# The scatter phase of a mixture-of-experts layer: W2 on 32x32 tiles of the matrix engine, block transposes on the vector engine

## The chip, the cores and the metric

The kernel runs on one core of one Trainium2 chip. The metric is the device time of one execution in microseconds. The engines are PE (matrix products; PEld is its weight load), DVE (vector), ACT (scalar), POOL (GpSimd) and SP, which here only issues transfers; 16 DMA engines move data.

## The reference

Tokens are 16,384 rows of 512. The output is `x + attention(xn) + ffn(xn)`, where `xn` is the layer norm of `x`. The attention part (a chunked state-space scan with projections) isn't touched except in how its result is stored. The feed-forward part is a mixture of 128 experts (32 x 4 sets) of inner size 32, in which each group of 32 consecutive tokens is treated by itself:

```
logits = einsum('bntd,des->bntes', grouped, Wc) + bc          # and a tiny tie breaker
perm = (logits == max over t)                                 # one-hot: each expert picks one token of the group
permuted = einsum('bntd,bntes->bnesd', grouped, perm)
inner = relu(einsum('bnesd,esdf->bnesf', permuted, W1) + b1)
result_permuted = einsum('bnesf,esdf->bnesd', inner, W2) + b2
result = einsum('bnesd,bntes->bntd', result_permuted, perm)   # back to the tokens that were picked
```

There are 512 groups. Everything is in fp32.

## The kernel before

Three phases follow each other. **Attention** runs over 64 tiles of 256 tokens and stores the normalised tokens (`xn_dram`), the residual sum (`part_dram`) and the one-hot rows (`permT_dram`, bf16). **Gather** runs over blocks of `GB` = 64 groups: PE picks each expert's token (`pick`, L1462), applies W1 (`apply_w1`, L1486), DVE clamps (`clamp_acc`, L1420), POOL adds b1 (L1376), and the inner results go to `inner_dram`. **Scatter**, which the change rewrites, applies W2 and b2 and sends the results back to the tokens.

The scatter works on `SG` = 128 groups at a time and a quarter of the 512 columns (`KD` = 4), 16 steps in all, each of `NW` = 8 units; there are 128 units. A unit has 16 experts:

- `apply_w2` (L1716): for each expert, W2 [32 inner x 128 columns] is the stationary operand and the inner results [32 x 128 groups] move; four experts lie on the four row tiles of PE. The result has columns on partitions and groups along the free axis.
- `add_b2` (L1693): DVE empties PSUM, adds b2 (here a per-partition value) and sorts into `resT[.., group, expert]`, two instructions of 1024 elements. For the first units ACT takes a quarter of it (`add_b2_last`, L1668).
- `transpose_results` (L1748), one step later: for each group PE transposes [128 columns x 128 experts], four into a PSUM bank, and ACT copies the bank (L1679) to `res`.
- `gather_results` (L1761): for each group `res` [128 experts x 128 columns] moves and the one-hot matrix `perm` [128 experts x 32 tokens] is stationary, on one of four column tiles.
- `write_out` (L1725): DVE adds the residual and SP stores (L1615).

SP issues the loads of W2 (L1576, one piece of 256 KB per unit), inner results (L1585), residual (L1612) and one-hot rows (L1589), which POOL unfolds from bf16 to fp32 (L1657). PE's order is written out by hand: the transposes of 16 groups, W2 of the unit `LAG` = 9 ahead, the 16 gathers:

```
for u in range(LAG, UNITS + LAG):
    first = UT * (u - LAG)
    for n in range(first, first + UT):
        transpose_results(n)
    if u < UNITS:
        apply_w2(pe, u)
    for n in range(first, first + UT):
        gather_results(n)
```

In the profile an fp32 product is two matmul instructions, one of type fp32r or a transpose is one. Tiles of the scatter have names that begin with `s_`, those of the gather with `g_`.

Of the kernel before, what the change touches and what calls it, by code (L numbers as in the profile page):

```python
# [55 lines left out]
SG = 128  # L56
NSET = TOK // (SG * GRP)
STL = SG * GRP // P
NW = 8
QW = NQ // NW  # L60

# [30 lines left out]
def attention_phase(nc, io, keep, sems):  # L92
# [250 lines left out]
    def sync_program(sync, gather):  # L343
# [877 lines left out]
def gather_phase(nc, io, keep, sems, att):  # L1221
# [25 lines left out]
    inner = [sb(f"inner{i}", [P, NQ, GB], at=AT_INNER + 8192 * i) for i in range(2)]  # L1247
# [78 lines left out]
    def store_inner(eng, b, piece):  # L1326

        quads = slice(PQ * piece, PQ * piece + PQ)
        eng.wait_ge(biased, 2 * b + 1 + 2 * piece // PIECES)
        eng.dma_start(inner_dram[b][:, quads, :], inner[b % 2][:, quads, :]).then_inc(inner_out[b % 2], 16)  # L1330

    def sync_program(sync, scatter):
# [10 lines left out]
        for e in range(4 * LAST):  # L1343
# [11 lines left out]
            if b == NGB - 1 and w % 4 == 3:  # L1355
                scatter["load_first"](sync, w // 4)
        for piece in range(PIECES // 2):
            store_inner(sync, NGB - 1, piece)
        for w in range(2):
            scatter["load_w2_next"](sync, w)  # L1360
        for piece in range(PIECES // 2, PIECES):
            store_inner(sync, NGB - 1, piece)
        for w in range(2, 4):
            scatter["load_w2_next"](sync, w)
# [5 lines left out]
    def gpsimd_program(pool):  # L1370
        for b in range(NGB):
            for i in range(2):
                pool.wait_ge(acc_cp, 2 * b + i + 1)
                quads = slice(2 * QW * i, 2 * QW * (i + 1))
                half = inner[b % 2][:, quads, :]
                nc.gpsimd.tensor_tensor(half, half, b1[:, quads].unsqueeze(2).to_broadcast([P, 2 * QW, GB]),  # L1376
                                        ALU.add).then_inc(biased, 1)
# [17 lines left out]
    def scalar_program(act, scatter):  # L1395
        for n in range(LAST):
            b, k = divmod(n, KD)
            for tq in range(2 if n == 0 else 0, 4):
# [10 lines left out]
                if b > 0 and 0 <= w - 5 < PIECES:  # L1409
                    store_inner(act, b - 1, w - 5)  # L1410
        for u in range(4):
            scatter["add_b2_last"](act, u)

    def vector_program(dve, scatter):
        def clamp_acc(b, i):
            dve.wait_ge(acc_ps, 4 * b + 2 * i + 2)
            if i == 0:
                wait(dve, inner_out[b % 2], 16 * PIECES * (b // 2))
            lower = b1neg[:, 2 * QW * i:2 * QW * (i + 1)].rearrange("p (j q) -> p j q", j=2)
            nc.vector.tensor_tensor(inner_view(b, i), acc_bank[:, halves(i), :, :],  # L1420
                                    lower.unsqueeze(3).to_broadcast([P, 2, QW, GB]), ALU.max).then_inc(acc_cp, 1)
# [96 lines left out]
def scatter_phase(nc, io, keep, sems, att, gat):  # L1518
# [11 lines left out]
    STEPS = NSET * KD  # L1530
    UT = STL // NW
    UNITS = STEPS * NW
    LAG = NW + 1
    EW = 4 * QW
    NC = 4
    CT = SG * GRP // NC
    NPART, NOUT = 2, 3

    w2 = sb("w2", [P, NW, QW, P], at=AT_XNT)
    b2 = sb("b2", [P, KD, EX], at=AT_PERM0)  # L1540
    ident = sb("ident", [P, P], at=AT_PERM0 + 2048)
    inner = sb("inner", [P, NQ, SG], at=AT_ONEHOT)
    permT = [sb(f"permT{i}", [P, CT], BF16, at=AT_PERM1 + 2048 * i) for i in range(2)]
    perm = sb("perm", [P, SG * GRP], at=AT_XN3)
# [340 lines left out]
```

## Time and profile before

| | |
|---|---|
| runs | 3000.07 us median of 3 (2998.5 to 3001.02) |
| profiled execution | 3002.6 us from the first to the last instruction |
| scatter, from the first transpose to the last gather product | 2488.7 to 2998.8 us |
| busy in the stretch 2485 to 3003 us (518 us) | PE 511, PEld 442, DVE 363, ACT 268, POOL 29 us; DMA 72% |
| busy in the gather phase, 2070 to 2480 us (410 us) | PE 319, PEld 274, DVE 181, ACT 148, POOL 29 us; DMA 46% |

The profile is one execution; its span is 2.5 us above the median of the runs. A line number (L1748) is a line of the kernel before. "Issue" as a releaser is time in which the engine waited for nothing that the profile shows. Busy time is the union of the instructions' durations; the mean of one is longer than the step between two where instructions overlap.

### The profile page before, as it was taken

What the parts mean: (1) busy time and instruction counts of PE and PEld (TensorE: products, weight loads), DVE (VectorE), ACT (ScalarE), POOL (GpSimd) and SP (SyncE); (2) the same over time, 40 slices, a digit from 0 to 9 for tenths busy, and PEclk for the clock granted to TensorE, in tenths of its full rate; (3) what the DMA queues carried; (4) which work ended last, traced back from release to release, by engine and by line L of the source; (5) the groups of instructions that cost most, each with busy time, mean ns of one, the idle gap of its engine ahead of it and who ended that gap; (6) DMA issues with size and microseconds to landing.
All of it is one profiled execution on the core that took longest, in us unless ns stands there. A gap on an engine that the chain in (4) does not pass through costs nothing.

```text
span 3002.6 us, 134681 instructions
## 1 busy us (share of the span) xinstructions
PE 2871.7 (96%) x59324; PEld 2453.1 (82%) x59324; DVE 2053.3 (68%) x2982; ACT 1713.5 (57%) x3751; POOL 1430.4 (48%) x2287
## 2 busy tenths in 40 slices
PE   8999999999999999999999999996787879999999
PEld 6888888888888888888888888885666668888887
DVE  5777777777777777777777777775444447777775
ACT  5665666666656666666566666663333335555555
POOL 4666676766666767667667666672010101101010
PEclk9999999999999999999999999998999999999999
DMA  4222222222222222222222222216444437877765
GB/s 150 77 74 71 77 78 75 76 74 77 74 71 79 76 76 76 70 80 74 72 79 74 80 71 71 81 46 214 131 134 119 115 110 217 235 218 223 225 206 156
DMA packets 372550, 328.99 MB, mean 110 GB/s; under 512 B 62960, under 2 KB 284656, under 8 KB 371328
## 3 DMA queue, kind: packets, MB, share of 16 engines
q1 hardware_dynamic: 362016, 310.21, 35.6%
q8 instruction: 469, 7.68, 1.1%
q10 hardware_dynamic: 9952, 10.17, 1.1%
q14 instruction: 113, 0.93, 0.1%
HBM read 206.96 MB, written 113.31 MB: 107 GB/s over the span
## 4 chain that ended last, share of the span: by engine, by line
PE 90%; DVE 4%; issue 3%; DMA 1%; SPq 1%; POOL 1%; ACT 0%; ACTq 0%; DVEq 0%; POOLq 0%
PE a_proj L992 40%; PE a_mix L992 11%; PE s_rt L1748 8%; PE g_pick_ps L1462 5%; PE a_scan L1106 5%; PE s_w_ps L1716 5%; PE s_rt L1761 4%; DVE g_picked L1393 3%; PE a_scan L1083 3%; PE a_scan L1070 2%; PE g_acc_ps L1486 2%; PE a_mix L1058 2%; PE a_misc L1050 1%; PE a_misc L1124 1%; DMA part_dram<-res 1%
## 5 line engine op out<-in xcount | busy, mean ns | idle before, releaser
L992 PE MATMUL a_proj<-wdh,xTh 128*128 128x512 f32 x1024 | 420.9, 411 | 5.0 <-issue 3.1
L1679 ACT COPY s_res<-s_rt 128x512 f32<-128x512 f32 x512 | 262.9, 601 | 245.8 <-PE s_rt L1748 245.8
L992 PE MATMUL a_proj<-wdh,xTl 128*128 128x512 f32 x1024 | 402.0, 393 | 0.0
L992 PE MATMUL a_proj<-wdl,xTh 128*128 128x512 f32 x1024 | 400.0, 391 | 1.5 <-issue 1.5
L824 DVE COPY_PREDICATED scan_in<-mask,a_scan 64x512 f32<-64x512 uint32 x512 | 382.3, 747 | 16.0
L1693 DVE TENSOR_TENSOR s_resT<-s_w_ps,s_b 128x1024 f32<-128x1024 f32 (+1 forms) x252 | 293.1, 1205 | 136.4 <-PE s_w_ps L1716 136.4
L465 POOL TENSOR_TENSOR dx<-xs,d_row 64x512 f32<-64x512 f32 x256 | 330.3, 1290 | 15.1
L640 ACT ACTIVATE scan_in<-CT,hsel 64x128 f32<-64x128 f32 x1024 | 326.0, 388 | 4.9
L473 POOL TENSOR_TENSOR yv<-yt,dx 128x512 f32<-128x512 f32 x128 | 188.6, 1473 | 292.8 <-DVE yt L864 292.8
L604 ACT ACTIVATE raw<-a_proj,rs 128x272 f32<-128x272 f32 x128 | 62.5, 488 | 427.6 <-PE a_proj L992 427.6
L1393 DVE COPY g_picked<-g_pick_ps 128x1024 f32<-128x1024 f32 x128 | 156.7, 1224 | 216.3 <-PE g_pick_ps L1462 216.3
L884 DVE SCALAR_TENSOR_TENSOR res<-a_mix,rms,x 128x512 f32<-128x512 f32 x127 | 95.4, 751 | 270.9 <-PE a_mix L992 258.6
L456 POOL TENSOR_TENSOR scan_in<-CT,hsel 64x512 f32<-64x512 f32 x256 | 269.0, 1051 | 10.0
L1389 ACT COPY g_picked<-g_pick_ps 128x1024 f32<-128x1024 f32 x128 | 129.6, 1012 | 248.4 <-PE g_pick_ps L1462 247.8
L1748 PE MATMUL s_rt<-s_ident,s_resT 128*128 128x128 f32 x2048 | 254.7, 278 | 0.9 <-DVE s_resT L1693 0.5
L616 ACT ACTIVATE xs<-a_proj,rs 64x512 f32<-64x512 f32 x256 | 174.8, 683 | 125.0 <-PE a_proj L992 123.4
L1748 PEld LDWEIGHTS s_rt<-s_ident,s_resT 128*128 128x128 f32 x2048 | 219.0, 140 | 31.6 <-issue 25.1
L992 PEld LDWEIGHTS a_proj<-wdh,xTh 128*128 128x128 f32 x1024 | 192.2, 188 | 47.5 <-issue 10.8
L992 PEld LDWEIGHTS a_proj<-wdh,xTl 128*128 128x128 f32 x1024 | 192.3, 188 | 45.4 <-issue 1.9
L992 PE MATMUL a_proj<-xTh,wth 128*128 128x256 f32 x768 | 222.1, 289 | 0.0
L992 PEld LDWEIGHTS a_proj<-wdl,xTh 128*128 128x128 f32 x1024 | 193.0, 188 | 35.2 <-issue 2.9
L992 PE MATMUL a_proj<-xTh,wtl 128*128 128x256 f32 x768 | 216.3, 282 | 0.0
(153 smaller groups left out, 7104.4 us busy)
## 6 DMA issues: line engine op xcount, KB each, us to landing
x<-in_x_dram SPq DMA_DIRECT2D x128, 256.0 KB, 2.7
xn_dram<-xn SPq DMA_DIRECT2D x128, 256.0 KB, 2.4
part_dram<-res SPq DMA_DIRECT2D x128, 256.0 KB, 2.5
g_xn<-xn_dram SPq DMA_DIRECT2D x512, 64.0 KB, 2.3
s_w<-in_w_dram SPq DMA_DIRECT2D x128, 256.0 KB, 4.1
s_part<-part_dram SPq DMA_DIRECT2D x128, 256.0 KB, 3.9
out_dram<-s_out SPq DMA_DIRECT2D x128, 256.0 KB, 3.0
xr<-in_xT_dram SPq DMA_DIRECT2D x126, 256.0 KB, 2.8
```

The source lines that it names most:

```text
L456: nc.gpsimd.tensor_tensor(c_places(1, w), src, sel, ALU.mult).then_inc(cs_cp[1], 1)
L465: nc.gpsimd.tensor_tensor(dx[rows_, :], xs[c][n % 4][rows_, :, :].rearrange("t h d -> t (h d)"), d_row[rows_, :], ALU.mult).then_inc(dx_cp, 1)
L473: nc.gpsimd.tensor_tensor(yv[:], yt[:], dx[:], ALU.add).then_inc(yv_cp, 1)
L616: last = nc.scalar.activation(xs[c][n % 4][rows_, :, :], proj[0][rows_, :].rearrange("p (h d) -> p h d", h=H), ACT.Copy, scale=inv(n, rows_))
L640: last = nc.scalar.activation(dst[:, :, j, :], CT[own, n % 4, :, 0:CH], ACT.Copy, scale=hsel4[own, j:j + 1])
L824: nc.vector.copy_predicated(dst, mask[rows_, :].unsqueeze(1).unsqueeze(1).to_broadcast([CH, 4, 2, CH]), src).then_inc(mt_cp, 1)
L992: last = nc.tensor.matmul(out, lhs[a], rhs[c], start=(k == 0 and n == 0), stop=(k == nk - 1 and n == 2))
L1106: last = nc.tensor.matmul(out, scan_in[c][:, h, i:i + 32], xs[c][n % 4][:, h, :], start=True, stop=True)
L1393: nc.vector.tensor_copy(picked_view(n, tq, 1), pick_view(1)).then_inc(pick_cp[1], 1)
L1679: nc.scalar.copy(res[:, n % 4, :, :], rt_bank[:, n % 3, :, :]).then_inc(res_cp, 1)
L1693: last = nc.vector.tensor_tensor(resT[m % 2][j][:, :, sets].rearrange("p n (q r) -> p n q r", r=4)[:, :, :, 0:r], w2_place(u)[:, 0:r, :, j ...
L1748: last = nc.tensor.transpose(rt_bank[:, n % 3, g, :], resT[m % 2][j][:, place, :], ident[:])
```

## The change

The scatter takes `SG` = 32 groups at a time and half of the columns (`NH` = 2, `DH` = 256): 32 steps of four units, 128 units as before. A unit has 32 experts.

- `apply_w2`: the inner results [32 inner x 32 groups] are the stationary operand and W2 [32 x 256 columns] moves. Row tile r holds expert r of a quad and column tile c another quad, so that the 16 tiles of 32 x 32 hold 16 experts. The result has groups on partitions (one column tile's experts in each 32) and columns along the free axis.
- `evict`: ACT copies it to `stage` in two instructions of 1024 elements, without b2.
- Once a step DVE turns `stage` into `turned` with four block transposes of 2048 elements per partition (`nc.vector.transpose` turns every 32 x 32 block of partitions and the innermost axis; both innermost axes step by 256 elements, 1 KB), after which experts are on partitions.
- `gather_results`: b2, split into two fp32r parts [128 experts x 256 columns], moves over the one-hot matrix of 128 tokens (four one-pass products a unit), and onto this sum the eight groups' gather products of 256 columns are added.
- ACT copies the sum out (`copy_out`), POOL adds the residual, SP stores.

W2's half (4 MB) stays in SBUF for 16 steps and is loaded twice in all. PSUM is used as three pairs of banks for W2 results and two banks for the output. In the gather phase the inner results are laid out in sets of 32 groups, so that the clamp and the addition of b1 are two instructions each in place of one. The residual is stored in halves of 256 columns. The core of the diff:

```diff
-SG = 128
+SG = 32
 NSET = TOK // (SG * GRP)
-STL = SG * GRP // P
-NW = 8
-QW = NQ // NW
+NH = 2
+DH = D // NH
...
+    inner = [sb(f"inner{i}", [P, GB // SG, NQ, SG], at=AT_INNER + 8192 * i) for i in range(2)]
...
+                for h in range(GB // SG):
+                    half = inner[b % 2][:, h, quads, :]
+                    last = nc.gpsimd.tensor_tensor(half, half, b1[:, quads].unsqueeze(2).to_broadcast([P, 2 * QW, SG]), ALU.add)
+                last.then_inc(biased, 1)
...
+            lower = b1neg[:, 2 * QW * i:2 * QW * (i + 1)].unsqueeze(2).unsqueeze(3)
+            for h in range(GB // SG):
+                last = nc.vector.tensor_tensor(inner_view(b, i, h), acc_view(i, h),
+                                               lower.to_broadcast([P, 2 * QW, GPT, SG // GPT]), ALU.max)
+            last.then_inc(acc_cp, 1)
...
-        w2_bank = ctx.enter_context(nc.psum_tensor("s_w2_ps", [P, 4, QW, SG], F32))
-        rt_bank = ctx.enter_context(nc.psum_tensor("s_rt", [P, 4, QW, SG], F32))
-    out_bank = rt_bank[:, 3, :, :].rearrange("p q n -> p (q n)")
+        bank = ctx.enter_context(nc.psum_tensor("s_ps", [P, 8, 2, DH], F32))
...
+    QB = 4
+    UNITS = NH * NSET * QB
+    STEPS = NH * NSET
+    LAG = 2 * QB
+    CT = SG * GRP
+    DT = DH // 4
+    NPART, NOUT, NINNER = 3, 3, 3
...
+    def pair(u, h):
+
+        first = h if u < 4 else (2 * u + h) % 3
+        return slice(2 * first, 2 * first + 2)
...
+        for u in range(UNITS + LAG + 1):
+            m, i = divmod(u, QB)
+            if u < UNITS and (m == NSET - 1 or i == QB - 1):
+                sync.wait_ge(w2_ps, u + 1)
+            if m == NSET - 1:
+                load_w2(sync, 1, i)
+            if i == QB - 1 and m + NINNER < STEPS:
+                load_inner(sync, m + NINNER)
+            v = u - LAG - 1
+            if v >= 0:
+                store(v)
+                if v + NPART < UNITS:
+                    load_part(v + NPART)
+                m, x = divmod(v, QB)
+                if x == 1 and m + 3 < STEPS:
+                    sync.wait_ge(perm_ready, m + 2)
+                    load_perm(sync, m + 3)
+            elif u == LAG - 1:
+                sync.wait_ge(perm_ready, 1)
+                load_perm(sync, 2)
...
+        def spread_perm(m):
+            pool.wait_ge(perm_in[m % 2], 16 * (m // 2 + 1))
+            wait(pool, out_ps, QB * (m - 1))
+            nc.gpsimd.tensor_tensor(perm[m % 2][:], permT[m % 2][:], ones[:].to_broadcast([P, CT]), ALU.mult).then_inc(perm_ready, 1)
...
+        for v in range(UNITS):
+            m, x = divmod(v, QB)
+            pool.wait_ge(out_cp, v + 1)
+            pool.wait_ge(part_in[v % NPART], 16 * (v // NPART + 1))
+            nc.gpsimd.tensor_tensor(out[v % NOUT][:], out[v % NOUT][:], part[v % NPART][:], ALU.add).then_inc(out_add, 1)
+            if x == 0 and m + 1 < STEPS:
+                spread_perm(m + 1)
...
+    def evict(act, u):
+
+        m, i = divmod(u, QB)
         act.wait_ge(w2_ps, u + 1)
-        for q in range(QW):
-            e = EW * w + 4 * q + 3
-            for j in range(2):
-                last = nc.scalar.activation(resT[m % 2][j][:, :, e], w2_place(u)[:, 3, q, j * GB:(j + 1) * GB],
-                                            ACT.Identity, bias=b2[:, m % KD, e:e + 1])
-        last.then_inc(res_last, 1)
+        wait(act, turn_cp, 4 * (m - 1))
+        places = stage[m % 2][:, 8 * i:8 * i + 8, :].rearrange("p (j r) d -> p r j d", r=4)
+        for h in range(2):
+            nc.scalar.copy(places[:, 2 * h:2 * h + 2, :, :], bank[:, pair(u, h), :, :]).then_inc(w2_cp, 1)
...
+        def copy_out(v):
+            act.wait_ge(out_ps, v + 1)
+            wait(act, out_done[v % NOUT], 16 * (v // NOUT))
+            nc.scalar.copy(out[v % NOUT][:], bank[:, 6 + v % 2, :, :]).then_inc(out_cp, 1)
...
+    def vector_program(dve):
+        for m in range(STEPS):
+            dve.wait_ge(w2_cp, 2 * QB * (m + 1))
+            wait(dve, out_ps, QB * (m - 1))
+            for y in range(4):
+                cols = slice(DT * y, DT * y + DT)
+                nc.vector.transpose(turned[m % 2][:, :, cols].rearrange("p n d -> p d n"),
+                                    stage[m % 2][:, :, cols].rearrange("p e d -> p d e")).then_inc(turn_cp, 1)
...
+    def apply_w2(pe, u):
+
+        m, i = divmod(u, QB)
+        k, s = divmod(m, NSET)
+        if s == 0:
+            pe.wait_ge(w2_in[i], 16 * (k + 1))
+        if i == 0:
+            pe.wait_ge(inner_in[m % NINNER], 16 * (m // NINNER + 1))
+        if u == 4:
+            pe.wait_ge(gat["acc_cp"], 2 * NGB)
+        wait(pe, w2_cp, 2 * u if u < 4 else 2 * u - 1)
+        for j in range(2):
+            for c in range(4):
+                for r in range(4):
+                    rows_ = slice(ES * r, ES * r + ES)
+                    dst = bank[32 * c:32 * c + 32, pair(u, r // 2), :, :][:, r % 2, j, :]
+                    last = nc.tensor.matmul(dst, inner[m % NINNER][rows_, 8 * c + 2 * i + j, :], w2[rows_, i, 2 * c + j, :],
+                                            start=True, stop=True)
+        last.then_inc(w2_ps, 1)
...
+        def gather_results(v):
+            m, x = divmod(v, QB)
+            cols = slice(m // NSET * DH, (m // NSET + 1) * DH)
+            if x == 0:
+                pe.wait_ge(perm_ready, m + 1)
+                pe.wait_ge(turn_cp, 4 * (m + 1))
+            wait(pe, out_cp, v - 1)
+            dst = bank[:, 6 + v % 2, :, :]
+            for t in range(2):
+                tile = slice((2 * x + t) * P, (2 * x + t + 1) * P)
+                for n in range(2):
+                    nc.tensor.matmul(dst[:, t, :], perm[m % 2][:, tile], b2[n][:, cols], start=(t == 0 and n == 0), stop=False,
+                                     skip_group_check=True)
+            for t in range(2):
+                for g in range(GPT):
+                    tok = (2 * x + t) * P + GRP * g
+                    last = nc.tensor.matmul(dst[GRP * g:GRP * g + GRP, t, :], perm[m % 2][:, tok:tok + GRP].bitcast(F32),
+                                            turned[m % 2][:, g * (SG // GPT) + 2 * x + t, :], start=False, stop=True,
+                                            skip_group_check=True)
...
+            for t in range(2):
+                for g in range(GPT):
+                    tok = (2 * x + t) * P + GRP * g
+                    last = nc.tensor.matmul(dst[GRP * g:GRP * g + GRP, t, :], perm[m % 2][:, tok:tok + GRP].bitcast(F32),
+                                            turned[m % 2][:, g * (SG // GPT) + 2 * x + t, :], start=False, stop=True,
+                                            skip_group_check=True)
             last.then_inc(out_ps, 1)
 
-        pe.wait_ge(small_in, 32)
-        for u in range(4, LAG):
-            apply_w2(pe, u)
-        for u in range(LAG, UNITS + LAG):
-            first = UT * (u - LAG)
-            for n in range(first, first + UT):
-                transpose_results(n)
+        pe.wait_ge(b2_lo, 1)
+        for u in range(4, UNITS + LAG):
             if u < UNITS:
                 apply_w2(pe, u)
-            for n in range(first, first + UT):
-                gather_results(n)
+            if u >= LAG:
+                gather_results(u - LAG)
...
-        w2=L0_ffn_W2.reshape(NW, QW, 4, KD, P, ES).transpose(3, 0, 2, 5, 1, 4).reshape(KD, NW, P, QW, P),
-        b2=L0_ffn_b2.reshape(EX, KD, P).transpose(2, 1, 0),
+        w2=L0_ffn_W2.reshape(4, 4, 2, 4, NH, DH, ES).transpose(4, 1, 3, 6, 0, 2, 5).reshape(NH, 4, P, 8, DH),
+        b2=L0_ffn_b2.reshape(EX, D),
```

## Rows read from the trace of the kernel before

**Rows 1.** The page: span, busy time by engine, granted clock in 40 slices, the chain.

```profile
span 3002.6 us, 134681 instructions
...
PE 2871.7 (96%) x59324; PEld 2453.1 (82%) x59324; DVE 2053.3 (68%) x2982; ACT 1713.5 (57%) x3751; POOL 1430.4 (48%) x2287
...
PEclk9999999999999999999999999998999999999999
...
PE 90%; DVE 4%; issue 3%; DMA 1%; SPq 1%; POOL 1%; ACT 0%; ACTq 0%; DVEq 0%; POOLq 0%
```

**Rows 2.** One tile, s_rt: count, ns min/median/max, first and last start.

```profile
L1761 PE MATMUL s_rt<-s_res,s_perm x4096: 269/273/298, 2492.3 to 2998.8; 128*32 128x128 f32 x196
...
L1748 PE MATMUL s_rt<-s_ident,s_resT x2048: 272/273/332, 2488.7 to 2997.5; 128*128 128x128 f32 x187
```

**Rows 3.** Windows of the gather and the scatter: busy time (matmuls), clock, DMA share, GB/s.

```profile
2070.00:2480.00 410.00, 319.32 (x12467) 274.21 (x12465) 180.89 (x152) 148.13 (x172) 28.53 (x15) 0.98 0.46 127
...
2485.00:3003.00 518.00, 510.98 (x10016) 441.56 (x10016) 362.93 (x373) 267.80 (x537) 28.67 (x16) 1.00 0.72 212
```

**Rows 4.** Timeline of the scatter, 2700 us: start, duration, engine, line, count.

```profile
2700.25 1.99 PE L1748 MATMUL s_rt<-s_ident,s_resT 128*128 128x128 f32 x16
2700.94 2.05 ACT L1679 COPY s_res<-s_rt 128x512 f32<-128x512 f32 x4 [1.98 <-PE s_rt L1748]
...
2702.17 1.17 PE L1716 MATMUL s_w_ps<-s_inner,s_w 32*128 32x128 f32 x32
...
2703.27 1.08 PE L1761 MATMUL s_rt<-s_res,s_perm 128*32 128x128 f32 x32
...
2704.28 1.99 PE L1748 MATMUL s_rt<-s_ident,s_resT 128*128 128x128 f32 x16
```

**Rows 5.** Timeline of PE in the attention phase, 1012 us.

```profile
1011.94 0.69 PE L1083 MATMUL a_scan<-cexp,BT 32*64 32x128 f32 x32
...
1013.29 0.28 PE L992 MATMUL a_proj<-xTh,wtl 128*128 128x256 f32 x1
1013.41 0.27 PE L992 MATMUL a_proj<-xTh,wth 128*128 128x256 f32 x1
```

**Rows 6.** What PE waited for in the gather phase: us in total, times, longest.

```profile
PE g_pick_ps L1462 <- DVE g_picked L1393: 36.9, 72, 9.1
PE g_acc_ps L1486 <- issue: 36.4, 41, 2.3
PE g_pick_ps L1462 <- issue: 10.2, 16, 1.6
```

**Rows 7.** Timeline of ACT in the gather phase.

```profile
2334.55 1.01 ACT L1389 COPY g_picked<-g_pick_ps 128x1024 f32<-128x1024 f32 x1
2335.45 1.02 ACT L1385 CAST g_perm<-g_acc_ps 128x1024 f32<-128x1024 bf16 x1
```

**Rows 8.** Groups by line and shape of DVE: busy us, mean ns of one.

```profile
L794 DVE STREAM_TRANSPOSE rsT<-rs 128x32 f32<-128x32 f32 x64 | 12.7, 199 | 0.0
...
L920 DVE TENSOR_TENSOR wtl<-a_misc,wth 128x64 fp32r<-128x64 f32 x1 | 0.2, 217 | 0.0
```

**Rows 9.** Groups by line and shape, gather and scatter, DVE and POOL.

```profile
L1693 DVE TENSOR_TENSOR s_resT<-s_w_ps,s_b 128x1024 f32<-128x1024 f32 x238 | 280.4, 1219 | 130.9 <-PE s_w_ps L1716 130.9
...
L1725 DVE TENSOR_TENSOR s_out<-s_rt,s_part 128x512 f32<-128x512 f32 x128 | 87.1, 681 | 21.0 <-PE s_rt L1761 21.0
...
L1376 POOL TENSOR_TENSOR g_inner<-g_inner,g_b 128x1024 f32<-128x1024 f32 x16 | 30.4, 1902 | 389.4 <-DVE g_inner L1420 389.4
L1657 POOL TENSOR_TENSOR s_perm<-s_permT,s_ones 128x1024 f32<-128x1024 bf16 x16 | 30.3, 1894 | 366.6 <-PE s_rt L1761 352.7 <-DMA s_permT<-permT_dram 13.8
...
L473 POOL TENSOR_TENSOR yv<-yt,dx 128x512 f32<-128x512 f32 x2 | 2.9, 1454 | 7.2 <-DVE yt L864 7.2
```

**Rows 10.** Transfers of the scatter: count, KB each, median us to landing.

```profile
s_part<-part_dram SPq DMA_DIRECT2D x128, 256.0 KB, 3.9
out_dram<-s_out SPq DMA_DIRECT2D x128, 256.0 KB, 3.0
```

**Rows 11.** Timeline, the last clamp of the gather phase.

```profile
2480.10 1.22 DVE L1420 TENSOR_TENSOR g_inner<-g_acc_ps,g_b1neg 128x1024 f32<-128x1024 f32 x1
```

More of the change, by code:

```diff
@@ L1354, in sync_program @@
                     load_xn(sync, e // 4 + 4, e % 4, i)
-            if b == NGB - 1 and w % 4 == 3:
-                scatter["load_first"](sync, w // 4)
-        for piece in range(PIECES // 2):
+            if b == NGB - 1:
+                scatter["load_first"](sync, w)
+        for piece in range(PIECES):
             store_inner(sync, NGB - 1, piece)
[L1359 to L1364, printed above, removed]
     def negate_b1(pool):
@@ L1537, in scatter_phase @@
[L1537 to L1544, printed above, removed]
-    resT = [[sb(f"resT{i}_{j}", [P, GB, EX], at=a + 32768 * i) for j, a in enumerate((AT_W1, AT_PICKED))] for i in range(2)]
-    res = sb("res", [P, 4, GPT, P])
@@ L1547, in scatter_phase @@
[L1547 to L1553 removed]
+    QB = 4
[5 more added lines that the diff above has]
+    NPART, NOUT, NINNER = 3, 3, 3
+    w2 = sb("w2", [P, QB, 8, DH], at=AT_W1)
@@ new lines, in scatter_phase @@
+    stage = [sb(f"stage{i}", [P, EX // 4, DH], at=a) for i, a in enumerate((AT_XNT, AT_W1 + 32768))]
+    turned = [sb(f"turned{i}", [P, SG, DH], at=AT_PICKED + 32768 * i) for i in range(2)]
+    inner = [sb(f"inner{i}", [P, NQ, SG], at=a) for i, a in enumerate((AT_PERM1, AT_PERM0, AT_XN3 + 12288))]
+    perm = [sb(f"perm{i}", [P, CT], F32R, at=AT_XN3 + 4096 * i) for i in range(2)]
+    permT = [sb(f"permT{i}", [P, CT], BF16, at=AT_XN3 + 8192 + 2048 * i) for i in range(2)]
+    b2 = [sb(f"b2{n}", [EX, D], F32R, at=AT_TOP + 2048 * i) for i, n in enumerate("hl")]
@@ L1554, in scatter_phase @@
+    b2_raw = sb("b2_raw", [EX, D], at=AT_TOP + 4096)
+    ones = sb("ones", [P, 1], at=AT_TOP + 6144)
+    part = [sb(f"part{i}", [P, 2, DH]) for i in range(NPART)]
+    out = [sb(f"out{i}", [P, 2, DH]) for i in range(NOUT)]
+    b2_in = sem("b2_in")
+    w2_in = [sem(f"w2_in{i}") for i in range(QB)]
+    inner_in = [sem(f"inner_in{i}") for i in range(NINNER)]
     perm_in = [sem(f"perm_in{i}") for i in range(2)]
@@ L1610, in sync_program, with load_first @@
+    def load_first(sync, w):
+        if w == 3:
+            sync.wait_ge(gat["perm_ps"], NGB)
+            sync.dma_start(b2_raw[:], io["b2"]).then_inc(b2_in, 16)
+            for m in range(2):
+                load_inner(sync, m)
+        if w in (8, 12):
+            for i in range(2):
+                load_w2(sync, 0, w // 2 - 4 + i)
+        if w == 15:
+            for m in range(2):
+                load_perm(sync, m)
+            load_inner(sync, 2)
     def sync_program(sync):
@@ new lines, in gpsimd_program, with round_b2 @@
+        for v in range(UNITS):
[5 more added lines that the diff above has]
+                spread_perm(m + 1)
+    def round_b2(act):
+        for i in range(2):
+            act.wait_ge(att["res_out"][i], 16 * NST)
+        act.wait_ge(b2_in, 16)
+        nc.scalar.copy(b2[0][:], b2_raw[:]).then_inc(b2_hi, 1)
@@ L1699, in apply_w2 @@
-    def apply_w2(pe, u):
-        m, w = divmod(u, NW)
-        pe.wait_ge(w2_in[w], 16 * (m + 1))
-        if m % KD == 0:
-            pe.wait_ge(inner_in[w], 16 * (SG // GB) * (m // KD + 1))
-        if u == 5:
-            pe.wait_ge(gat["acc_cp"], 2 * NGB)
-        elif 5 < u < LAG:
-            pe.wait_ge(res_ready, u - 1)
-            pe.wait_ge(res_last, u - 1)
-        else:
-            wait(pe, res_ready, u)
-            wait(pe, res_last, min(u, LAG))
-        for j in range(QW):
-            for r in range(4):
-                rows_ = slice(ES * r, ES * r + ES)
-                last = nc.tensor.matmul(w2_place(u)[:, r, j, :], w2[rows_, w, j, :], inner[rows_, QW * w + j, :],
-                                        start=True, stop=True)
-        last.then_inc(w2_ps, 1)
@@ L1720, in vector_program @@
[L1720 to L1726 removed]
         for u in range(4, UNITS + LAG):
             if u < UNITS:
[L1730 removed]
+                evict(act, u)
```

194 lines of the change are left out of this document (39 added, 155 removed).

## The prediction

> **What bounds the kernel now.** I read the page first [rows 1]: 3002.6 us of span, PE busy for 96% of it at full granted clock, and the chain that ended last is 90% PE. That share is an average over three phases, so the groups by line and the windows by stage came next. The change rewrites the last phase, the scatter, which by the last two of its PE lines runs from 2488.7 us to the end [rows 2], 510 us of PE work from the first transpose to the last gather product (2998.8). In this phase PE is busy for 511 of 518 us, DVE for 363, ACT for 268 and the DMA engines for 72% [rows 3]; everyone waits for PE, and PE for nobody. A timeline shows what a unit is made of [rows 4]: 16 transposes (L1748), then 16 W2 products (L1716, two instructions each), then 16 gather products (L1761, two each). They start at 2700.25, 2702.17, 2703.27, and the next unit at 2704.28: a unit takes 4.03 us, 1.92 of them for transposes, 1.10 for W2, 1.01 for gathering. There are 128 of them, 3.985 us each on average.
>
> **How PE's time scales.** Four numbers come from [rows 4, 5]. Transposes: 15 gaps in 1.99 - 0.27 = 1.72 us, 0.115 each, one at a time. Products on four tiles (L1761): 32 starts in 1.08 - 0.27 = 0.81 us; in bursts of four that is 7 gaps of 0.116, so 128 fp32 columns occupy the four tiles for about 0.11 us and the four run together. Products on eight tiles (32 rows by 64 columns, L1083): 32 starts in 0.69 - 0.27 = 0.42 us, 3 to 4 gaps of 0.11: eight run together. A change from one tile shape to another: L1761's last start is 0.81 us after its first and the next transpose starts at 1.01, so 0.20 from last start to next start, of which 0.11 is streaming and 0.09 the change; a first burst costs up to 0.1 more (L1716 needs 0.90 us for the same 7 gaps).
>
> **The change, part by part.** *PE.* The 2048 transposes go: 1.92 us a unit. W2 now has 32 products (64 instructions) of 256 columns on sixteen tiles of 32 by 32. If sixteen run together as eight do in [rows 5], a burst of 16 lasts twice 0.109, 0.218 us, and a unit has four: the last start comes 3 x 0.218 + 0.2 (slower first burst, spread of the starts) = 0.85 us in, the next stage 0.218 + 0.09 later: 1.16 us. The bias has four one-pass products of 256 columns on the whole array; the same size starts every 0.117 us in the attention phase (1013.29, 1013.41) [rows 5]: 3 x 0.117 + 0.05 + 0.117 + 0.09 = 0.61 us. Eight gather products of 256 columns are four bursts: 3 x 0.218 + 0.05 + 0.31 = 1.01 us. A unit: 1.16 + 0.61 + 1.01 = 2.78 us in place of 3.985.
>
> The Trainium skill has a measurement for sixteen tiles (TensorE: Matmul & The Clock Gate, Part 3: Packing small matmuls, Measured speedup vs the span model): 4x4 packing gains 10.6 times, not 16. By that, a W2 burst would be an estimated 0.33 us instead of 0.218, the unit 3.2 us and the kernel some 50 us above my sum, at the upper edge of the forecast. No row of before has sixteen tiles.
>
> *Issue waits.* PE stands still for no reason that the profile shows ("issue") 57 times for 46.6 us in the gather phase [rows 6] with its 12,467 matmuls in 410 us [rows 3], 3.7 ns a matmul; in the scatter it practically never does, with 10,016 in 518 us. Without its waits on "issue" and on DVE the gather issued 12,467 / (410 - 87) = 39 a us, the old scatter 19, the new unit has 64 + 4 + 16 = 84 in 2.78 us, 30. On the line between (19, 0) and (39, 3.7) that is about 2.1 ns a matmul; 10,750 matmuls make 23 us. Bounds: 0 and 3.7 ns (40 us).
>
> *ACT* takes both evictions of W2 (two of 1024 elements) and the copy-out (512). Back to back, a 1024-element ACT copy starts 0.90 us after the last (2334.55, 2335.45) [rows 7] and a 512-element one 0.48 (four in 2.05 us, 0.60 the last, [rows 4]): 2 x 0.90 + 0.48 + some 0.1 of waiting = 2.4 us a unit. It hides behind PE's 2.78 with little to spare, and is the floor if PE proves faster. PE's next W2 waits only for the first eviction, 1.1 us after the products, behind 1.62 us of bias and gather.
>
> *DVE* turns experts to partitions: four block transposes of 2048 elements a step (four units), and nothing else. Before has such an instruction only at 32 elements, 199 ns, next to a 64-element tensor op of 217 [rows 8]: 217 less 64 elements at DVE's pace (1219 - 681 ns for 512 more, 1.05 ns each [rows 9]) leaves 150 fixed, so 199 leaves room for at most 1.5 ns an element. At 1.05 ns a transpose is 2.15 + 0.08 = 2.2 us, 8.9 us a step against PE's 11.1: hidden. But the source and the destination of the new ones step 1 KB from element to element, and no DVE row steps so through SBUF. From below 2.2 us; from above I take double, 4.4. I take 2.2, since DVE's own reads in L1693, whose innermost step is a whole PSUM bank, keep 1.05 ns.
>
> *POOL* adds the residual: 512 elements, between half of the 1.90 us of L1376 and the 1.45 of L473 [rows 9], 1.0 to 1.5 us a unit, and one unfold of 1.89 us in four units (L1657): at most 2.0 a unit, hidden. *DMA:* W2 is loaded twice in all instead of 128 times; a unit moves 256 KB in, 256 out, 128 of inner results and 64 of one-hot rows, 704 KB in place of about 860, in pieces of 1 KB and more where the store had 512 B. In 2.9 us that is 240 GB/s; before had 212 at a share of 0.72 [rows 3]. Hidden; the output ring of three gives a store 3 x 2.78 less its own 0.5, some 7.8 us, for the add (1.5), at worst an unfold (1.9) and a landing (3.0 [rows 10]). SP issues fewer transfers than before. In the gather phase the clamp and the bias add are split in two, 16 clamps at 2 x 681 against 1214 ns: at most 2.4 us.
>
> *Ends.* The last clamp is over at about 2481.4 [rows 11]; DVE's first step of transposes then ends at 2481.4 + 8.9 = 2490.3, while ACT empties units 4 to 8 at 1.95 each: the first gather is at 2490.5. It takes 1.6, then 119 full units x 2.78 = 331, issue waits 23. Then eight gathers of 1.62 = 13.0, with a wait of 2.8 for the last four (the last transposes end 2.0 + 8.9 us after the last W2, five gathers take 8.1). Copy, add and store: 4.9. Sum: 2490.5 + 1.6 + 331 + 23 + 15.8 + 4.9 + 2.4 = 2869 us of span against 3002.6. The runs shown have their median at 3000.07, 2.5 below that: 2867.
>
> **The rivals.** *DVE becomes the bound (slower than before).* If a strided transpose takes two steps an element, 4.35 us, a scatter is 128 x 4.35 = 557 us from 2481.4, then four gathers and the end, 11.4: 3050, or 3047 by the runs' scale. It decides from 3002.6 - 11.4 - 2481.4 = 510 us / 128 = 3.98 us a transpose upwards. For it: nothing in before has this access. Against it: [rows 8] and the PSUM reads. Chance 0.13. The Trainium skill speaks for this one (SBUF — State Buffer, Door 1: The DMA port swizzle): SBUF has lines of 16 bytes and an access that moves to a new line each time pays a penalty, which every element of these transposes does. No row of before shows it.
>
> *Tiles don't run sixteen together.* With eight at a time W2 needs eight bursts, 0.87 us more a unit, 119 x 0.87 = 104 us, less the issue waits: 2950; for it, before never has more than eight. With this go heavier issue waits (10 ns a matmul, nearly three times the gather's, would be 108 us). Together 0.13, 2925 to 2990. With only four at a time W2 costs 2.6 us more a unit and the kernel 3155: chance 0.03, since [rows 5] speak against it.
>
> *ACT is the only bound, and issue waits vanish.* 119 x 2.4 instead of 2.78, and no 23 us: 2799. Chance 0.10 for 2799 to 2825.
>
> **How the numbers follow.** The forecast of 2867 (2825 to 2925: units of 2.6 to 3.1 us with the issue waits between their bounds) 0.60; faster still 0.10; eight tiles or more waiting 0.13; DVE slow 0.13; four tiles 0.03; no change 0.01. Against a bound of 0.2% (about what a measurement of this kernel can tell from no change): faster 0.83, same 0.01, slower 0.16. The range is 2810 to 2985 and leaves out the two slow cases and the fastest edge, 2 in 10; the likeliest case alone has 2825 to 2925.
>
> **What would show it.** W2 products in bursts of 16 and some 1.2 us a unit; no s_rt transposes; PE near 95% with the scatter over by 2870. DVE's transposes at 2.2 us with some 2 us of idle time a step before them that ends on ACT; at 4.3 us, and PE waiting for DVE in each fourth gather, the prediction is wrong. PE waiting for ACT evictions in every unit would say that ACT sets the pace. Gaps of about 1 us before PE instructions put down to "issue" are the term of 23 us.

## The result: slower, with DVE as the bound

The changed kernel takes 3038.61 us in the median (3036.05 to 3042.7, 4 runs) against 3000.1 (2998.5 to 3001.02, 4 runs) before: ratio 1.0123, 95% interval 1.0111 to 1.0135. The forecast was 2867. It went the way of the first rival, "DVE becomes the bound", which had its price at 3047, its turning point at 3.98 us a transpose, and a chance of 0.13.

The page of the changed kernel, for [rows 1]: span, busy time, DVE and the granted clock in 40 slices, the chain.

```profile
span 3035.2 us, 135365 instructions
...
PE 2799.8 (92%) x59836; PEld 2250.2 (74%) x59836; DVE 2220.8 (73%) x2743; ACT 1749.4 (58%) x3552; POOL 1628.4 (54%) x2447
...
DVE  6777777777777777777777777774444449999998
...
PEclk9999999999999999999999999998999979998988
...
PE 87%; issue 6%; DVE 4%; DMA 1%; SPq 1%; POOL 1%; ACT 0%; POOLq 0%; ACTq 0%; DVEq 0%
```

By the whole span PE still looks like the bound (92%). The DVE line says otherwise: in the slices that lie wholly in the scatter it has 9, and 8 in the last. The windows of the gather and the scatter, for [rows 3], make it plain:

```profile
2070.00:2480.00 410.00, 324.01 (x12637) 277.09 (x12636) 176.23 (x162) 150.35 (x150) 30.83 (x30) 0.97 0.46 134
2485.00:3035.00 550.00, 437.44 (x10432) 239.54 (x10432) 534.51 (x127) 305.35 (x376) 222.24 (x159) 0.88 0.56 175
```

In the scatter PE went from 511 of 518 us busy to 437 of 550, DVE to 535 of 550, and the granted clock from 1.00 to 0.88. The gather phase before it ends within 1 us of where it did (last clamp at 2480.6 instead of 2481.3). The groups by line, from the page, for [rows 9] (busy us, mean ns | idle time before, and what ended it):

```profile
L1700 DVE STREAM_TRANSPOSE s_turned<-s_stage 128x2048 f32<-128x2048 f32 x128 | 539.0, 5225 | 2.0 <-ACT s_stage L1678 2.0
...
L1678 ACT COPY s_stage<-s_ps 128x1024 f32<-128x1024 f32 x256 | 247.1, 1018 | 210.5 <-DVE s_turned L1700 107.6
...
L1657 POOL TENSOR_TENSOR s_out<-s_out,s_part 128x512 f32<-128x512 f32 x128 | 164.8, 1288 | 325.6 <-ACT s_out L1684 324.5
```

The mean of 5.2 us is not the time from one transpose to the next: neighbouring transposes overlap in their records. That time, called the pace or the step of DVE below, is busy time by count, 539.0 / 128 = 4.21 us, and DVE was idle for 2.0 us in all. DVE starts at 2480.5, and 2480.5 + 539.0 + 2.0 = 3021.5; four gathers, adds and stores make the remaining 13.7 us of the 3035.2. The whole time after the gather phase is accounted for by one line.

What PE does meanwhile, in a timeline of PE, ACT and DVE at 2700 us, for [rows 4]:

```profile
2692.51 22.22 DVE L1700 STREAM_TRANSPOSE s_turned<-s_stage 128x2048 f32<-128x2048 f32 x5
...
2701.89 1.93 ACT L1678 COPY s_stage<-s_ps 128x1024 f32<-128x1024 f32 x2 [3.67 <-DVE s_turned L1700]
2701.90 0.36 PE L1735 MATMUL s_ps<-s_b2h,s_perm 128*128 128x256 f32 x1 [3.05 <-issue]
...
2702.70 1.94 PE L1740 MATMUL s_ps<-s_turned,s_perm 128*32 128x256 f32 x16
...
2704.57 1.93 PE L1719 MATMUL s_ps<-s_w,s_inner 32*32 32x256 f32 x64
...
2706.43 0.39 PE L1735 MATMUL s_ps<-s_b2h,s_perm 128*128 128x256 f32 x1
...
2707.10 1.07 PE L1740 MATMUL s_ps<-s_turned,s_perm 128*32 128x256 f32 x16
...
2708.10 1.49 PE L1719 MATMUL s_ps<-s_w,s_inner 32*32 32x256 f32 x64
...
2709.53 0.39 PE L1735 MATMUL s_ps<-s_b2h,s_perm 128*128 128x256 f32 x1
```

Once in four units PE stands still for about 3 us in front of the bias, the first instruction behind its wait on the transposes' count (30 times, 93.8 us in all, between 2500 and 3020 us). The profile names no releaser there ("issue"), but ACT, which waits on the same count, starts 0.01 us earlier and names DVE. Reading only the names, one would have blamed PE's instruction stream. After the stop PE's next gather and W2 stages take 1.87 and 1.86 us from start to start, and then 1.00 and 1.43 again. Windows over the two pairs of stages give the reason (the granted clock is the third number from the end):

```profile
2702.70:2706.40 3.70, 3.70 (x81) 1.59 (x80) 3.70 (x2) 1.71 (x3) 1.03 (x1) 0.59 0.04 11
2707.10:2709.50 2.40, 2.40 (x81) 1.23 (x80) 2.40 (x2) 1.86 (x3) 1.87 (x2) 1.00 0.71 214
```

After the idle time PE is granted 0.59 of full speed, mostly the 1.2 GHz level, and then 2.4 GHz again. Between two waits this costs nothing, since PE waits for DVE anyway. It does cost at the very end, where nothing is left to hide it: after 8.2 us of idle time the first two of the last four units, which have only bias and gather, take 2.99 and 2.52 us (granted 0.50 and 0.61) where the third takes 1.67, some 2.2 us in all.

### The profile page after: what moved, and what is told of

Same layout as the page of the kernel before. It is cut to its first block, busy times and chain, and to the rows that moved or that the text cites. A ratio compares the mean times of both kernels' runs of the same rounds, so it can differ in the third digit from the quotient of the medians.

```text
span 3035.2 us, 135365 instructions
## 1 busy us (share of the span) xinstructions
PE 2799.8 (92%) x59836; PEld 2250.2 (74%) x59836; DVE 2220.8 (73%) x2743; ACT 1749.4 (58%) x3552; POOL 1628.4 (54%) x2447
## 4 chain that ended last, share of the span: by engine, by line
PE 87%; issue 6%; DVE 4%; DMA 1%; SPq 1%; POOL 1%; ACT 0%; POOLq 0%; ACTq 0%; DVEq 0%
PE a_proj L991 39%; PE a_mix L991 11%; PE s_ps L1719 6%; PE g_pick_ps L1465 5%; PE a_scan L1105 5%; PE s_ps L1740 5%; PE s_ps L1735 3%; DVE g_picked L1394 3%; PE a_scan L1082 3%; PE a_scan L1069 2%; PE g_acc_ps L1489 2%; PE a_mix L1057 2%; PE a_misc L1049 1%; PE a_misc L1123 1%; DMA part_dram<-res 1%
## 5 line engine op out<-in xcount | busy, mean ns | idle before, releaser
L1700 DVE STREAM_TRANSPOSE s_turned<-s_stage 128x2048 f32<-128x2048 f32 x128 | 539.0, 5225 | 2.0 <-ACT s_stage L1678 2.0
L1678 ACT COPY s_stage<-s_ps 128x1024 f32<-128x1024 f32 x256 | 247.1, 1018 | 210.5 <-DVE s_turned L1700 107.6
L1657 POOL TENSOR_TENSOR s_out<-s_out,s_part 128x512 f32<-128x512 f32 x128 | 164.8, 1288 | 325.6 <-ACT s_out L1684 324.5
L1377 POOL TENSOR_TENSOR g_inner<-g_inner,g_b 128x512 f32<-128x512 f32 x32 | 32.9, 1049 | 382.9 <-DVE g_inner L1423 382.9
L1719 PE MATMUL s_ps<-s_w,s_inner 32*32 32x256 f32 x8192 | 208.4, 421 | 11.6 <-ACT s_stage L1678 10.0
```

The lines of the kernel that those rows point to most:

```text
L1657: nc.gpsimd.tensor_tensor(out[v % NOUT][:], out[v % NOUT][:], part[v % NPART][:], ALU.add).then_inc(out_add, 1)
L1678: nc.scalar.copy(places[:, 2 * h:2 * h + 2, :, :], bank[:, pair(u, h), :, :]).then_inc(w2_cp, 1)
L1700: nc.vector.transpose(turned[m % 2][:, :, cols].rearrange("p n d -> p d n"), stage[m % 2][:, :, cols].rearrange("p e d -> p d e")).then_in ...
L1719: last = nc.tensor.matmul(dst, inner[m % NINNER][rows_, 8 * c + 2 * i + j, :], w2[rows_, i, 2 * c + j, :], start=True, stop=True)
```

## Experiments

Ratios are to the kernel before, measured on the same chip beside each run; on the chips of these runs it takes 3005 to 3006 us. Steps of DVE are busy time over 128.

### One transpose side at a time

**e1_dense**: both sides of the transpose run through contiguous memory; all else stays, so the values land in other places. L1700 and the next line become, in short,

```python
nc.vector.transpose(turned_flat[:, 2048*y:2048*y+2048],   # 64 rows of 32, contiguous
                    stage_flat[:, 2048*y:2048*y+2048])
```

> The block transposes read and write 2048 consecutive elements instead of steps of 1 KB; the same count and size, the values land in other places (the result is not the reference's), all else as in the changed kernel. Theory A (the step of 1 KB costs the time): a transpose starts every 2.2 us instead of 4.21, DVE is hidden, PE sets the pace at the 3.10 us a unit that it shows between its waits, span about 2885 us, ratio to before about 0.96. Rival B (a block transpose of fp32 takes two steps an element whatever the layout): 4.2 us and 3035 us as in the changed kernel.

Measured: 2924.91 us, ratio 0.9731 (0.9695 to 0.9766), as theory A has it for the transposes. The span, 2920.0, is 35 us above the 2885 expected: the first gather starts late and PE has issue waits here too (see the last part of "Why the prediction was wrong"), and the gather phase of this execution ends 6 us later. **e2_src_strided** keeps the source as the change has it (1 KB from element to element) and makes the destination contiguous; **e3_dst_strided** is the reverse.

> As the dense one, but the source keeps its step of 1 KB and only the destination is dense (values in other places). Theory A1 (strided reads cost): 4.2 us a transpose, about 3035 us. A2 (strided writes cost): 2.2 us, about 2885 us. B: 4.2 us.

> As the dense one, but the destination keeps its step of 1 KB and only the source is dense (values in other places). A1: 2.2 us a transpose, about 2885 us. A2: 4.2 us, about 3035 us. If both sides cost, this and the kernel with only the source strided are both at 4.2 us, or both between 2.2 and 4.2 if the two add.

Measured: 2981.17 (ratio 0.9918, 0.9889 to 0.9947) and 2976.06 (0.9901, 0.9871 to 0.9931). The groups by line of the three, e1, e2 and e3 in this order, each from its own page:

```profile
L1700 DVE STREAM_TRANSPOSE s_turned<-s_stage 128x2048 f32<-128x2048 f32 x128 | 284.5, 2280 | 137.5 <-ACT s_stage L1678 137.5
```

```profile
L1700 DVE STREAM_TRANSPOSE s_turned<-s_stage 128x2048 f32<-128x2048 f32 x128 | 476.9, 3996 | 4.0 <-ACT s_stage L1678 4.0
```

```profile
L1700 DVE STREAM_TRANSPOSE s_turned<-s_stage 128x2048 f32<-128x2048 f32 x128 | 469.9, 4027 | 4.1 <-ACT s_stage L1678 4.1
```

Contiguous, a transpose takes 284.5 / 128 = 2.22 us, the 2.2 of the prediction; with either side stepping 3.73 and 3.67; with both 4.21. So each long step by itself takes the pace from 1.1 to about 1.8 ns an element, and the second adds only 0.5 us more. Both sides cost, which is the last case that I had written down for e3, except that the two do not add. DVE's idle time shows the bound moving: 137.5 us with both contiguous, 4 with one.

### Who pays for the step

**e4_act_turns** moves the source's step to ACT, which then writes each element 128 bytes from the last (the 32 expert places of one column lie between), so that DVE reads contiguously.

```diff
-    stage = [... [P, EX // 4, DH] ...]
+    stage = [... [P, DH, EX // 4] ...]
-        places = stage[m % 2][:, 8 * i:8 * i + 8, :].rearrange("p (j r) d -> p r j d", r=4)
+        places = stage[m % 2][:, :, 8 * i:8 * i + 8].rearrange("p d (j r) -> p r j d", r=4)
```

> The evictions on ACT write the results of W2 with the experts innermost (steps of 128 bytes between columns), so that DVE reads its source densely; the destination keeps its step of 1 KB. The result is the reference's. A1 (reads alone cost): DVE at 2.2 us; ACT pays if a strided write costs it as much: 2 x 1.7 + 0.5 = 3.9 us a unit and about 2990 us, or nothing (2.4 us a unit, PE sets the pace, 2885 us). A2 or B: DVE stays at 4.2 us, 3035 us or more.

Measured: 3033.53, ratio 1.0092 (1.0063 to 1.0121). DVE takes 3.70 us, as in e3; ACT's copies doubled. The groups of both in the list by line of e4, and what PE waited for from 2500 to 3000 us:

```profile
L1678 ACT COPY s_stage<-s_ps 128x1024 f32<-128x1024 f32 x256 | 488.3, 2029 | 17.6 <-PE s_ps L1719 11.8 <-DMA inner_dram<-g_inner 5.8
L1700 DVE STREAM_TRANSPOSE s_turned<-s_stage 128x2048 f32<-128x2048 f32 x128 | 474.1, 3834 | 56.4 <-ACT s_stage L1678 56.4
```

```profile
PE s_ps L1719 <- ACT s_stage L1678: 114.2, 120, 2.0
```

and its window of 2500 to 2900 us (ACT is the fourth engine), where ACT is busy for 398 of 400:

```profile
2500.00:2900.00 400.00, 308.08 (x8144) 172.23 (x8141) 355.04 (x97) 397.83 (x290) 165.67 (x118) 0.98 0.58 183
```

The step was handed to another engine, which pays more for it than DVE saves. ACT's copy takes 2029 ns against 1018; by busy time that is (488.3 - 247.1) / 32 = 7.5 us more in a step. DVE saves (539.0 - 474.1) / 32 = 2.0 us in a step, because the destination still steps. ACT is now the bound: PE waits for it in each unit. I had expected 3.9 us a unit and 2990 us if ACT pays; a unit takes 4.1.

### Two elements side by side

**e5_pairs** keeps the transposes and changes the layouts: pairs of neighbouring columns stay together in `stage` and in `turned`, so that two fp32 (8 bytes) lie side by side. ACT and the gather take both; DVE, whose blocks need expert after expert of one column, steps 8 bytes from element to element, two of them in 16 bytes.

```diff
-    stage = [... [P, EX // 4, DH] ...]
-    turned = [... [P, SG, DH] ...]
+    stage = [... [P, DH // 2, EX // 4, 2] ...]
+    turned = [... [P, DH // 2, SG, 2] ...]
...
-                nc.vector.transpose(turned[m % 2][:, :, cols].rearrange("p n d -> p d n"),
-                                    stage[m % 2][:, :, cols].rearrange("p e d -> p d e")).then_inc(turn_cp, 1)
+                nc.vector.transpose(turned[m % 2][:, DT // 2 * y:DT // 2 * (y + 1), :, :].rearrange("p c n b -> p c b n"),
+                                    stage[m % 2][:, DT // 2 * y:DT // 2 * (y + 1), :, :].rearrange("p c e b -> p c b e")).then_inc(turn_cp, 1)
```

ACT's eviction and the gather's moving operand are indexed to match.

> Both buffers hold two columns side by side (stage as [column pair][expert][2], turned as [column pair][group][2]), so that a transpose steps by 8 bytes on both sides; ACT writes and PE reads runs of two elements 256 bytes apart. The result is the reference's. Theory C (only a long step costs; neighbours within 16 bytes don't): a transpose starts every 2.2 us, ACT's evictions and PE's gather products keep 0.90 and 1.00 us, PE sets the pace as with dense transposes, ratio about 0.973. Theory D (any step over one element costs): DVE stays at 3.7 to 4.2 us, ratio 0.99 to 1.01. If ACT pays for its runs of two (1.9 us an eviction as with single elements): 4.3 us a unit, ratio 1.01. The Trainium skill (SBUF — State Buffer, Door 1: The DMA port swizzle) speaks for C: two hits on a 16-byte line are enough for full bandwidth.

Measured: 2919.96 us (2913.62 to 2926.4, 4 runs), ratio 0.9729 (0.9703 to 0.9756): the whole computation, 2.7% faster than the kernel before. Its DVE and ACT groups and its waits of 2510 to 2880 us:

```profile
L1701 DVE STREAM_TRANSPOSE s_turned<-s_stage 128x2048 f32<-128x2048 f32 x128 | 290.9, 2333 | 130.6 <-ACT s_stage L1678 130.6
...
L1678 ACT COPY s_stage<-s_ps 128x1024 f32<-128x1024 f32 x256 | 271.5, 1123 | 99.1 <-PE s_ps L1720 92.1 <-DMA inner_dram<-g_inner 7.0
```

```profile
DVE s_turned L1701 <- ACT s_stage L1678: 117.0, 29, 6.5
ACT s_stage L1678 <- PE s_ps L1720: 70.2, 112, 2.3
...
PE s_ps L1720 <- issue: 9.3, 12, 1.3
```

The step of DVE is 290.9 / 128 = 2.27 us, against 2.22 contiguous. DVE now waits for ACT and ACT for PE, so PE sets the pace, as the forecast had it. ACT's copy pays 10% for writing in pairs (1123 ns for 1018), which hides. PE's gather stage, whose moving operand now has pairs 256 bytes apart, keeps its 1.00 us. **e6_pairs_src** and **e7_pairs_dst** have the pairs on one side alone.

> Only the source has pairs (step 8 bytes, ACT writes runs of two); the destination keeps its step of 1 KB. The result is the reference's. Theory C: as with a dense source, 3.67 us a transpose, ratio about 0.990. Theory D: 4.2 us, ratio about 1.012.

> Only the destination has pairs (step 8 bytes, PE's gather products read runs of two 256 bytes apart); the source keeps its step of 1 KB. The result is the reference's. Theory C: 3.73 us a transpose, ratio about 0.992, and gather products of 1.00 us a unit. Theory D: 4.2 us, ratio about 1.012. If PE reads runs of two at half pace, its gather stage is 1.9 us; hidden here behind DVE, but 4.0 us a unit when both sides have pairs.

Measured: 2979.44 (0.992, 0.9899 to 0.9942) and 2990.2 (0.9952, 0.9937 to 0.9968). DVE's groups of e6 and e7, each from its own page:

```profile
L1701 DVE STREAM_TRANSPOSE s_turned<-s_stage 128x2048 f32<-128x2048 f32 x128 | 475.6, 4687 | 4.4 <-ACT s_stage L1678 4.4
```

```profile
L1700 DVE STREAM_TRANSPOSE s_turned<-s_stage 128x2048 f32<-128x2048 f32 x128 | 482.9, 3841 | 4.1 <-ACT s_stage L1678 4.1
```

The steps are 3.72 and 3.77 us. Pairs on one side are worth what contiguous elements on that side are (e3 with 3.67, e2 with 3.73), within 0.1 us, and both sides are needed.

What the runs can't tell is how far two elements may lie apart. They have steps of 4 and 8 bytes, which are cheap, and of 128 bytes (on ACT) and 1 KB, which are dear; no run has a step between 8 and 128 bytes. They do show that a long step between pairs is cheap (ACT, 256 bytes from pair to pair), so it is not the length of the step alone that costs.

### What W2 costs

With DVE out of the way, PE's unit is 3.10 us where I forecast 2.78; the larger part is W2's stage, 1.43 where I had 1.16. The timeline of e5 shows it, in a stretch in which PE works without a gap:

```profile
2705.61 1.07 PE L1741 MATMUL s_ps<-s_turned,s_perm 128*32 128x256 f32 x16
2706.61 1.49 PE L1720 MATMUL s_ps<-s_w,s_inner 32*32 32x256 f32 x64
...
2708.70 1.07 PE L1741 MATMUL s_ps<-s_turned,s_perm 128*32 128x256 f32 x16
```

**e8_rows_outer** exchanges W2's two inner loops in e5; **e9_split_cols** splits each of its products in two.

```diff
-            for c in range(4):
-                for r in range(4):
+            for r in range(4):
+                for c in range(4):
```

```diff
-                    last = nc.tensor.matmul(dst, ..., w2[rows_, i, 2 * c + j, :], start=True, stop=True)
+                    for f in range(2):
+                        half = slice(DH // 2 * f, DH // 2 * (f + 1))
+                        last = nc.tensor.matmul(dst[:, half], ..., w2[rows_, i, 2 * c + j, half], start=True, stop=True)
```

> The paired layout on both sides of the transposes (2920 us in the last call), and in W2's product loop the order of the two inner loops exchanged: the row group r outside, the column group c inside. The computation is the same. A W2 stage takes 1.43 us from its first start to the bias's first, where I forecast 1.16; its first three bursts of sixteen start 0.216 us apart as forecast, and the last one's starts are spread out. Theory S: what holds W2 up is that 64 instructions each need about 17 ns to start, whatever tile they go to. Then the order changes nothing: stage 1.43 us, unit 3.10, time within 0.3% of 2920. Theory O: it is the order, four neighbouring products share a column group and must be drained together before the next stage's tiles are free. Then the stage falls towards 1.16 us, the unit to some 2.85, and the time by up to 120 x 0.25 = 30 us, to about 2890. A dearer order (each group of four now writes another bank) would show a stage longer than 1.43.

> The paired layout on both sides, and each of W2's 32 products of 256 columns split into two of 128 columns: the same columns stream through the same tiles, in 128 instructions a unit instead of 64. The computation is the same. Theory S (about 17 ns a start sets the stage): the stage becomes 128 x 0.017 + 0.3 = some 2.5 us, the unit 4.15, and the time 120 x 1.05 = 125 us more than 2920, about 3045. Theory F (streaming sets it, 8 bursts of 0.109 us in place of 4 of 0.218): stage 1.3 to 1.5 us, time 2915 to 2945. In between, a longer stage with starts closer than 17 ns, would say that both have a part.

Measured: e8 2934.6 us, ratio 0.9761 (0.9726 to 0.9796), which can't be told from e5's 0.9729 (the intervals overlap). Its undisturbed W2 stages keep 1.49 us of duration and 1.42 from start to start, so theory O is out for this order. e9 3142.13, ratio 1.0452 (1.0423 to 1.048). A unit of e9 in the timeline:

```profile
2708.78 2.71 PE L1722 MATMUL s_ps<-s_w,s_inner 32*32 32x128 f32 x128
2711.41 0.39 PE L1738 MATMUL s_ps<-s_b2h,s_perm 128*128 128x256 f32 x1
...
2712.08 1.07 PE L1743 MATMUL s_ps<-s_turned,s_perm 128*32 128x256 f32 x16
2713.09 2.71 PE L1722 MATMUL s_ps<-s_w,s_inner 32*32 32x128 f32 x128
```

The stage is 2711.41 - 2708.78 = 2.63 us: 64 more starts for the same columns cost 1.21 us, 18.9 ns each on average. The streaming theory, 1.3 to 1.5 us, is out; the number of instructions counts.

Theory S, a fixed time for each start whatever tile it goes to, is not shown by this. The 18.9 ns are a mean. In e5's stage at 2706.61, 32 of the 64 instructions start within the first 0.37 us, in bursts about as forecast, and the other 32 between 2707.07 and 2707.73, most of them 17 ns apart. And the time is not fixed: e9's stage at 2497.49, at a granted clock of 0.50, lasts 4.45 us where those at 1.00 last 2.71. Each start also has its own weight load, and e9 puts twice as many instructions in a row on the same tile. What part each of these has stays open.

The total of e9 was 97 us above my expectation. Of the 224 us between the two profiled spans, 119 units x 1.21 are 144 and the later first gather (bias at 2515.0 instead of 2499.6) 15; PE's waits on "issue" rose from 11 to 33 us in the window 2510 to 2880, which makes some 40 more over the scatter. The rest, about 25 us, is not accounted for.

## Why the prediction was wrong

**The step that failed** is "I take 2.2, since DVE's own reads in L1693, whose innermost step is a whole PSUM bank, keep 1.05 ns". The pace of reads of PSUM did not carry over to SBUF, and on its SBUF side L1693 writes four experts next to each other, so it has no single elements there. Contiguous, the 2.2 us is right to 1% (e1), but the layouts of the change make it 4.21 (e2, e3: each side has a part; e5: a step of 8 bytes takes it away). It was within the bounds that I had set, 2.2 to 4.4 us, with the turning point at 3.98 between them. With no row of this access in the profile, values spread evenly between the bounds would have given 0.42 / 2.2 = 0.19 for one beyond 3.98, where I gave 0.13.

A second fault is in how the prediction counts: 3.98 us is where the kernel becomes slower than before, but DVE becomes the bound much earlier, once four transposes take longer than PE's four units, at 2.78 us, or 2.97 with the issue waits. Between the two the forecast of 2867 is wrong as well, and this stretch had no price. By my own sum for rival 1, 2481.4 + 128 x 3.7 + 11.4 - 2.5 = 2964 us at 3.7; e2 and e3, which have 3.73 and 3.67, measured 2981 and 2976.

Rival 1 gave 3050 us of span: 557 of transposes (measured 539, 4.21 instead of 4.35) and 11.4 for the end (13.7, 2.2 more of it at the low clock). So that rival had the mechanism and nearly the size: PE waits for DVE once in four units. The forecast's own case failed.

The kernel before had one access of this kind, which the prediction passes over: for nine of its units ACT writes single elements 512 bytes apart (L1668). At 64 elements an instruction and with records that overlap it gives no price.

The Trainium skill states a rule that fits this (SBUF — State Buffer, Door 1: The DMA port swizzle; also Advanced Engine Details and Errata, SBUF Cachelines): lines of 16 bytes, and at least two hits on one are needed to absorb the latency of the access. The runs agree: single fp32 elements 128 bytes or 1 KB apart pay on DVE's reads, on its writes and on ACT's writes; with two in 16 bytes DVE pays 2% (2.27 against 2.22 us) and ACT 10%. That the line has 16 bytes no run here shows; anything above 8 and up to 128 bytes would fit them.

**The rest, point by point**, read where DVE is out of the way (e5, span 2911.8 against the forecast's 2869):
- *W2 mis-sized*: 1.42 to 1.43 us instead of 1.16. The first 33 starts come about as forecast (0.46 us instead of 0.44); from there to the last it takes 0.66 us instead of 0.41. It is still less than eight tiles at a time would give (1.16 + 0.87 = 2.03), so that rival did not come true. *Bias* 0.67 instead of 0.61, *gather* 1.00 (1.01). A unit is 3.10 instead of 2.78, and 119 of them are 38 us.
- *Issue waits*: 119 units take 388.3 us from 2502.63 to 2890.97, 19.4 more than 119 x 3.10; PE's list has 11.1 us of "issue" in them (and 2.8 later, the wait for the last transposes, as forecast). The other 8 us I did not trace. The term was 23.
- *The start*: e5's first gather stage begins at 2499.61 instead of 2490.5 (in the changed kernel 2500.56), 9.1 us, and takes 3.0 instead of 1.6. The 2.4 us that my sum had for the split clamps, at its end, did not come: the last clamp is over at 2479.0 (2480.6 in the changed kernel), not after 2481.4. The timeline of the changed kernel there shows two things that I left out:

```profile
2486.66 1.93 ACT L1678 COPY s_stage<-s_ps 128x1024 f32<-128x1024 f32 x2 [6.78 <-DMA inner_dram<-g_inner]
...
2487.72 2.38 PE L1719 MATMUL s_ps<-s_w,s_inner 32*32 32x256 f32 x64 [5.42 <-ACT s_stage L1678]
...
2490.14 1.93 ACT L1678 COPY s_stage<-s_ps 128x1024 f32<-128x1024 f32 x2 [1.55 <-PE s_ps L1719]
...
2491.21 2.38 PE L1719 MATMUL s_ps<-s_w,s_inner 32*32 32x256 f32 x64 [1.11 <-ACT s_stage L1678]
```

  ACT's first eviction after the gather phase begins only at 2486.66, because ACT's program waits in front of it for all stores of inner results (my sum let ACT begin at 2481.4). Then PE and ACT take turns, since the next unit's products wait for ACT's first copy of the unit before, at 3.48 us a unit, 2.38 of it PE's part at a granted clock of 0.50 (1.2 GHz), where I had 1.95.
- *The end* takes 20.8 us from the last full unit against 15.8 + 4.9 = 20.7. In all 9.1 - 2.4 (clamps) + 1.4 + 38 - 3.6 (issue waits) + 0.1 = 42.6 us, the 42.8 between the spans: without DVE's step the time would have been at 2920, inside the likeliest case's range (2825 to 2925) but at its edge, as its unit of 3.10 us is the upper end of the 2.6 to 3.1 that the range allowed.
- *ACT* (two copies in 1.93 us and 0.59 for the copy-out, 2.5 us a unit by busy time for the 2.4 forecast) and *POOL's add* at 1.29 us were sized rightly and are hidden, and so is *DMA* (busy for 74% from 2510 to 2880 us, 234 GB/s). ACT never became the only bound, since PE's unit is longer than forecast.
- *Sixteen tiles*: the measurement in the Trainium skill (TensorE: Matmul & The Clock Gate, Measured speedup vs the span model), 10.6 times for sixteen tiles, pointed the right way: the estimate from it was a unit of 3.2 us and 50 us above my sum; the runs have 3.10 and 43, of which W2 is 119 x 0.27 = 32. The same section of the Trainium skill models the span of one set of tiles as one product and some 4 ns for each tile more. In the long row of products here the mean is 18.9 ns for each start more (e9), so that model can't be carried over to such a row.

## What to carry to other kernels

Ask of each access to SBUF how many elements it takes side by side; where it takes single fp32 elements with long steps, look for a layout that keeps pairs together before moving the step to another engine. When no row shows the access on which a rival hinges, the chance comes from where its turning points lie between the bounds, and there are two: where the other engine becomes the bound, and where the change becomes a loss. When small tiles run in parallel, count starts as well as columns.

## What the runs showed that I had not expected

- A 2048-element fp32 block transpose on DVE: 2.22 us contiguous, 3.67 to 3.77 with one side taking single elements, 4.21 with both, 2.27 with 8-byte pairs on both. The two sides do not add up (1.5 + 1.5 would give 5.2), and one cured side alone leaves 3.7.
- ACT, evicting 1024 fp32: 1018 ns contiguous, 1123 in pairs, 2029 as single elements 128 bytes apart.
- On sixteen 32x32 tiles, 64 more instructions for the same columns cost 18.9 ns each on average, though single starts come much closer together. The two orders of the tiles that were run cost the same.
- A wait for DVE can stand in the chain as "issue" of PE. The engine that waits on the same count shows who it was.
